# A fused vision block: which PSUM bank each matmul step writes, by strict turn or by an account of when banks are read

## The chip, the cores and the metric

The kernel runs on one core of a Trainium2 chip. The time is the device time of one execution in microseconds. Three executions of the kernel before took 4943.49, 4945.65 and 4948.21 us, so its median is 4945.65 us. Each further execution that was profiled has a span, from its first to its last instruction.

## The reference, cut to what matters

64 images of 3 x 224 x 224 and 64 texts of 77 x 64 come in; 861 tokens of 64 features per image go out. All of it is float32.

```python
p = x.reshape(B, 3, 28, 8, 28, 8).transpose(0, 2, 4, 1, 3, 5).reshape(B, 784, 192)
h = p @ W_embed + b_embed + sin_positional_encoding(784, 64)
for i in range(3):                                  # graph of the 28 x 28 grid
    hw = h @ W_gcn[i]
    agg = hw * snorm; agg = agg.at[:, dst].add(hw[:, src] * enorm)
    h = relu(agg + b_gcn[i])
h = concatenate([h @ W_out + b_out, txt], axis=1)   # 784 + 77 = 861 tokens
a = layernorm(h)
h = h + attention(a)          # 4 heads of 16, softmax over 861 keys, bf16 before Wo
m = layernorm(h)
h = h + shared_mlp(m) + top2_of_4_experts(m)        # 64->64->128->64; 64->128->64->64
```

## The kernel before, in words

The work of an image is cut into steps: tuples such as `("s", g, half, kb, head)`. One list of steps is made on the host for 16 pairs of images at a time (`windows`, `window`), and all five engines walk through that same list in its order, each doing its own part of every step. So the list is the program order of every engine at once. Between the two lists of 16 pairs, all engines meet and the semaphores are cleared.

Where a step stands in the list is set by constants, not by a planner: `image_steps` and `pair_steps` give each group of steps a start and an end in units of images, relative to the image's own scores (0 to 1), `spread` lays the group's steps evenly between them by a rough cost, and `window` sorts everything by that place. With a period of two images, each constant that is a pair of pairs has one value for even and one for odd images. `PACK`, `GRAPH`, `FETCH` place the work of the pair that is coming, up to six images ahead of its scores.

The steps that matter here, with the lines of the profile:

- `s` (PE L1217, one matmul of 432 columns; ScalarE L889 takes the exponential out of PSUM), 56 per image; `pv` (PE L1227, four column groups at once into banks 4 and 5).
- `mx` (PE L1239, one matmul of 432 columns; VectorE L1004 takes the row maximum), 56 per image: the softmax's maximum for the coming image.
- `qk` (PE L1289; ScalarE L910 writes the high part; the step `qkl`, VectorE L1072, then reads the same bank again for the low part) and `gw` (PE L1262; ScalarE L896, then `gwl`, VectorE L1026): banks with two readers, one after the other.
- `gagg` (PE L1271, VectorE L1043), `xt` (PE L1277, ScalarE L905), `v` (PE L1299, VectorE L1082 and L1084), `ot` (PE L1305, VectorE L1091 and L1092), `obt` (PE L1310), `wo` (PE L1316, VectorE L1099), `l1` (PE L1289, ScalarE L952), `l2` (PE L1325 and L1327, ScalarE L958), `wt` (PE L1332, ScalarE L938), `wb` (PE L1339, VectorE L1183), `l3` (PE L1348, ScalarE L962 and L963), `back` (PE L1353, VectorE L1190 and L1191), `embed` (PE L366, VectorE L1018).
- Without PSUM: `xc` (GpSimd L361), the layer norm steps (GpSimd L820 to L837), the expert biases `hb` (GpSimd L847, L852, L857), and the transfers `load`, `fetch`, `text`, `scratch`, `stack` and `store` on the SyncE queue.

PSUM has eight banks. Banks 4 and 5 hold the attention output. The other six, 0, 1, 2, 3, 6 and 7, serve all other matmul steps. `turns` gives each such step its bank: strictly the next of the six. It also gives the number of the bank's use. Before TensorE starts a step it waits until the bank's former user has been read (`pe.wait_ge(free[r], prior)`); every reader waits for `full[r]`. All engines call `turns` on the same list, so they agree.

Of the kernel before, what the change touches and what calls it, by code (L numbers as in the profile page):

```python
# [86 lines left out]
def spread(steps, start, end):  # L87

    def cost(st):
        if isinstance(st, list):  # L90
            return sum(cost(one) for one in st)
        return WAIT * st[1] if st[0] == "wait" else COST.get(st[0], 1)

    total, passed, out = sum(cost(st) for st in steps), 0, []
    for st in steps:
        at = start + (end - start) * passed / total
        out += [(at, one) for one in (st if isinstance(st, list) else [st]) if one[0] != "wait"]
        passed += cost(st)
    return out


def attention_steps(g):
    units = [(half, kb) for half in range(2) for kb in range(NB)]
    out, due = [], []
    for n, unit in enumerate(units):
        for h in range(HEADS):
            out.append(("s", g, *unit, h))
            if h == 1:
                out += due
                due = []  # L110
                if n and n % 2 == 0:
                    out.append([("pv", g, *one) for one in units[n - 2:n]])
                    due = [("oev", g, half) for half, kb in units[n - 2:n] if kb == NB - 1]
    return out + [[("pv", g, *one) for one in units[2 * NB - 2:]], ("wait", 0.1), ("oev", g, 1)]


def max_steps(g):
    out, due = [], []
    for qb in range(NB):
        for h in range(HEADS):  # L120
            for half in range(2):
                out.append(("mx", g, qb, h, half))
                out += due[:1] if half else []
                due = due[1:] if half else due
        due += {3: [("nm", g, 0), ("mrow", g, 0), ("mload", g, 0)],
                NB - 1: [("nm", g, 1), ("mrow", g, 1), ("mload", g, 1)]}.get(qb, [])
    return out + [due[0], ("wait", 0.2), due[1], ("wait", 0.2), due[2]]


def norm_steps(g, which):  # L130

    out = []
    for k in ("sum", "mean", "ln", "wait", "sq", "wait", "var", "ln2", "wait", "scale", "hi", "lo"):
        out.append(("wait", 0.1) if k == "wait" else (k, g, which))
    return out


def finish_steps(g):
    return [("ot", g, 0), ("ot", g, 1), ("wait", 1), ("obt", g), ("wait", 1), ("wo", g)]
# [6 lines left out]
def gate_steps(g):  # L146
    return [("wait", 0.1) if k == "wait" else (k, g) for k in GATE_CHAIN]


def expert_steps(g):  # L150

    out = [("xt", g, "m", 0), ("xt", g, "m", 1), ("wait", 1), ("gate", g)]
    for e in range(EXPERTS + 1):
        out += [("l1", g, e, 0), ("l1", g, e, 1)]
        out += {2: [[("l2", g, 0, 0), ("l2", g, 0, 1)]], 4: [[("l2", g, 1, 0), ("l2", g, 1, 1)]]}.get(e, [])
    return out + [("wt", g), ("l2", g, 2, 0), ("l2", g, 2, 1),
                  [("wb", g, 0, 0), ("wb", g, 0, 1), ("wb", g, 1, 0), ("wb", g, 1, 1)], ("wait", 1), ("l3", g), ("wait", 1),
                  ("back", g)]
# [2 lines left out]


MAX = ((-0.694, 0.158), (-0.638, 0.168))
FINISH = ((0.995, 1.063), (0.994, 1.097))
NORM_M = ((1.109, 1.257), (1.123, 1.197))
EXPERT = ((1.374, 1.997), (1.267, 1.882))
GATE = ((1.492, 1.665), (1.347, 1.379))
BIAS = ((1.602, 1.796), (1.435, 1.621))
NORM_A = ((-1.472, -1.34), (-1.504, -1.457))
PROJECT = ((-1.307, -1.281), (-1.361, -1.284))  # L170
STACK = ((-1.018, -0.911), (-1.082, -0.936))
VALUE = (-0.952, -0.989)

GRAPH = (-2.075, -1.519)
PACK = (-4.037, -3.674, -3.438, -2.779)
VGAP = 0.154
STORE = (2.456, 2.503)
FETCH = -5.787
LOAD_LEAD, EMBED_LAG = 0.117, 0.217


def image_steps(g):
# [3 lines left out]
    def part(steps, times):  # L186
        return spread(steps, g + times[b][0], g + times[b][1])

    project = [("xt", g, "a", 0), ("xt", g, "a", 1), ("wait", 1), ("qk", g, 0), ("qk", g, 1), ("wait", 0.2), ("qkl", g, 0),
               ("qkl", g, 1), ("scratch", g)]  # L190
    return (spread(attention_steps(g), g, g + 1.0) + part(max_steps(g), MAX) + part(finish_steps(g), FINISH)
            + part(norm_steps(g, "m"), NORM_M) + part(expert_steps(g), EXPERT) + part(gate_steps(g), GATE)
            + part([("hb", g, n) for n in range(2 * EXPERTS + 1)], BIAS) + part(norm_steps(g, "a"), NORM_A)
            + part(project, PROJECT) + part([("stack", g, n) for n in range(STACK_PARTS)], STACK)
            + [(g + VALUE[b], ("v", g, 0)), (g + VALUE[b] + VGAP, ("v", g, 1)), (g + STORE[b], ("store", g))])


def pair_steps(p):
# [7 lines left out]
    out = [(t - 1.8, ("text", p))] + spread(graph + [("gw", p, 3, 0), ("gw", p, 3, 1)], t + GRAPH[0], t + GRAPH[1])  # L206
    out.append((t + FETCH, ("fetch", p)))
    for q in range(4):
        out += [((t + PACK[q - 1] if q else t - 2 + PACK[3]) + LOAD_LEAD, ("load", p, q)), (t + PACK[q], ("xc", p, q)),
                (t + PACK[q] + EMBED_LAG, ("embed", p, q))]  # L210
    return out
# [16 lines left out]
def windows(pairs):  # L228
# [4 lines left out]
    while at < pairs:  # L233
# [6 lines left out]
ROTATING = ("s", "embed", "gw", "gagg", "mx", "mrow", "ot", "obt", "wo", "xt", "qk", "v", "gate", "l1", "l2", "wt", "wb", "l3",  # L240
            "back")


def turns(steps):

    count, out = {}, {}
    turn = 0
    for st in steps:
        if st[0] in ROTATING:
            bank = (0, 1, 2, 3, 6, 7)[turn % 6]  # L250
            turn += 1
        elif st[0] == "pv" and st[3] == 0:
            bank = 4 + st[2]
        else:
            continue
        count[bank] = count.get(bank, 0) + 1
        out[st] = (bank, count[bank], count[bank] - 1)
    return out
# [30 lines left out]
def build(nc, pairs, x, txt, edges, plain, split, rows, const, out):  # L289
    ctx = ExitStack()  # L290
    with ctx:
# [400 lines left out]
        def _(sp):  # L692
            def run(steps, base, init):
                turn, nth = turns(steps), ordinal(steps)
                packed_last = latest(steps, "xc")
                for st in steps:
# [69 lines left out]
        def _(pool):  # L766
# [17 lines left out]
            def run(steps, base, init):  # L784
                chain[0] = 0
                made.clear()
                turn, nth = turns(steps), ordinal(steps)
                embed_last = latest(steps, "embed")
                xt_last, lo_last = latest(steps, "xt"), latest(steps, "lo")
# [76 lines left out]
        def _(act):  # L866
            def run(steps, base, init):
                turn, nth = turns(steps), ordinal(steps)
                scratch_last = latest(steps, "scratch")
                hb_no = ranks(steps, lambda st: st[0] == "hb" and st[2] == 2 * EXPERTS)  # L870
# [560 lines left out]
```

## Time and profile before

| | before |
|---|---|
| median of 3 runs | 4945.65 us |
| the profiled execution, its own time | 4939.67 us |
| its span | 4937.9 us |
| mean granted TensorE clock | 0.981 |
| PE (matmul) busy | 4719.4 us, 96% |
| PEld (weight load) busy | 3135.6 us, 64% |
| DVE (VectorE) busy | 3206.6 us, 65% |
| ACT (ScalarE) busy | 2979.3 us, 60% |
| POOL (GpSimd) busy | 1696.6 us, 34% |

Matmuls are pipelined: one of 432 columns is recorded as lasting 0.35 to 0.36 us, and yet the next can start about 0.19 us after it. A TensorE that is shown as busy can therefore still be late between two matmuls. The rows of PEld, the weight loads, are the finer gauge: every matmul has its load, and a load that comes late has its idle time and its releaser beside it.

### The profile page before, as it was taken

How to read it: one execution, taken by the hardware profiler on the slowest of the kernel's cores; microseconds unless marked ns; L12 is line 12 of the kernel's file. 1: busy time of each engine (PE TensorE's matmuls, PEld its weight loads, DVE VectorE, ACT ScalarE, POOL GpSimd, SP SyncE). 2: the span in 40 equal slices, each digit the busy share in tenths (PEclk: the TensorE clock that was granted, in tenths of full speed). 3: DMA queues.
4: the chain of work that ended last, by engine and by line, in shares of the span. 5: the costliest groups of instructions: out<-in, count | busy, mean ns of one | idle time of the engine just before them, and what ended most of it. 6: DMA issues, size and time to landing. Idle time of an engine off the chain costs nothing.

```text
span 4937.9 us, 80911 instructions
## 1 busy us (share of the span) xinstructions
PE 4719.4 (96%) x29262; PEld 3135.6 (64%) x29262; DVE 3206.6 (65%) x7342; ACT 2979.3 (60%) x6161; POOL 1696.6 (34%) x1681
## 2 busy tenths in 40 slices
PE   6599999999999999999999999999999999999997
PEld 4466666666666666666666666666666666666654
DVE  4366666676666666666666666667666667666663
ACT  0156666666566666666656666666666666656665
POOL 3123333334234333334333334333333333423322
PEclk8699999999999999999999999999999999999998
DMA  2433433433433432443332443333333343343220
GB/s 87 102 78 81 87 83 78 90 74 81 87 84 77 90 76 74 90 85 82 81 78 70 90 85 82 80 81 75 82 86 82 80 88 74 83 85 74 34 48 6
DMA packets 193397, 385.98 MB, mean 78 GB/s; under 512 B 74986, under 2 KB 118634, under 8 KB 193002
## 3 DMA queue, kind: packets, MB, share of 16 engines
q1 hardware_dynamic: 191978, 379.91, 34.2%
q8 instruction: 237, 3.88, 0.4%
q14 instruction: 158, 1.29, 0.1%
q10 hardware_dynamic: 1024, 0.89, 0.1%
HBM read 309.13 MB, written 109.26 MB: 85 GB/s over the span
## 4 chain that ended last, share of the span: by engine, by line
PE 74%; DVE 11%; ACT 7%; issue 2%; DMA 2%; POOL 1%; ACTq 0%; SPq 0%; DVEq 0%; another core or an unknown queue 0%; POOLq 0%
PE ps L1227 15%; PE ps L1217 13%; PE ps L1239 12%; PE ps L1271 9%; DVE neg_max_halves L1004 8%; PE ps L1289 6%; PE ps L1327 4%; ACT probs L889 4%; PE ps L1348 3%; PE ps L1262 3%; PE ps L366 2%; PE ps L1277 2%; PE ps L1316 2%; PE ps L1295 1%; DMA image_rows<-image_by_row 1%
## 5 line engine op out<-in xcount | busy, mean ns | idle before, releaser
L1004 DVE TENSOR_REDUCE neg_max_halves<-ps 123x1 f32<-123x432 f32 (+1 forms) x3584 | 2000.9, 598 | 766.9 <-PE ps L1239 751.9
L889 ACT ACTIVATE probs<-ps 123x432 f32<-123x432 f32 x3584 | 1690.9, 542 | 663.7 <-PE ps L1217 626.8
L1239 PE MATMUL ps<-k_stack,q_stack 96*123 96x432 f32 x3584 | 1293.5, 396 | 38.5 <-DMA k_stack<-qk_scratch 22.3
L1217 PE MATMUL ps<-q_stack,k_stack 97*123 97x432 f32 x3584 | 1253.1, 395 | 52.6 <-ACT probs L889 12.5
L1239 PEld LDWEIGHTS ps<-k_stack,q_stack 96*123 96x123 f32 x3584 | 638.7, 186 | 419.1 <-issue 273.2
L1217 PEld LDWEIGHTS ps<-q_stack,k_stack 97*123 97x123 f32 x3584 | 641.8, 186 | 340.1 <-issue 107.7
L1227 PE MATMUL ps<-probs,v_and_one 123*32 123x432 f32 x7168 | 763.3, 540 | 1.6 <-ACT probs L889 1.6
L952 ACT ACTIVATE hidden<-ps,plain_w 128x432 f32<-128x432 f32 x640 | 400.2, 634 | 148.2 <-PE ps L1289 148.2
L1271 PE MATMUL ps<-adjacency,parts_hi 112*128 112x392 f32 x1344 | 463.5, 345 | 3.5 <-DVE parts_lo L1026 3.4
L1271 PE MATMUL ps<-adjacency,parts_lo 112*128 112x392 f32 x1344 | 459.8, 342 | 0.0
L815 POOL TENSOR_TENSOR nodes_T<-nodes_T,dinv_row 128x392 f32<-128x392 f32 x128 | 130.8, 1023 | 846.4 <-ACT nodes_T L901 845.3
L1227 PEld LDWEIGHTS ps<-probs,v_and_one 123*32 123x32 f32 x7168 | 182.5, 110 | 353.5 <-issue 287.2
L820 POOL TENSOR_TENSOR centred_and_squared<-tokens,ln_stats_m 123x448 f32<-123x448 f32 x64 | 59.9, 936 | 980.0 <-DVE ln_stats_m L1058 980.0
L852 POOL TENSOR_TENSOR moe_T<-gate_weights,bias_rows 123x448 f32<-123x448 f32 x256 | 242.9, 949 | 311.9 <-DVE gate_weights L1160 283.3
L1043 DVE TENSOR_TENSOR nodes_T<-ps,dinv_row 128x392 f32<-128x392 f32 x192 | 108.4, 565 | 323.3 <-PE ps L1271 323.3
L857 POOL TENSOR_TENSOR tokens<-tokens,moe_T 123x448 f32<-123x448 f32 x256 | 292.6, 1143 | 32.4
L820 POOL TENSOR_TENSOR centred_and_squared<-tokens_next,ln_stats_a 123x448 f32<-123x448 f32 x64 | 59.9, 935 | 674.7 <-DVE ln_stats_a L1058 674.7
L361 POOL COPY patch_columns<-image_rows 96x392 f32<-96x392 f32 x256 | 235.3, 948 | 94.1 <-DMA image_rows<-image_by_row 73.4
L958 ACT ACTIVATE hidden<-ps,plain_w 128x492 f32<-128x492 f32 (+1 forms) x384 | 234.1, 634 | 51.7 <-PE ps L1327 43.7
L1271 PEld LDWEIGHTS ps<-adjacency,parts_hi 112*128 112x128 f32 x1344 | 255.3, 190 | 6.2 <-issue 3.9
L1262 PE MATMUL ps<-plain_w,nodes_T 128*112 128x128 f32 (+2 forms) x1792 | 243.2, 278 | 14.8 <-POOL nodes_T L815 6.8
L1271 PEld LDWEIGHTS ps<-adjacency,parts_lo 112*128 112x128 f32 x1344 | 255.4, 190 | 1.6
(158 smaller groups left out, 6118.3 us busy)
## 6 DMA issues: line engine op xcount, KB each, us to landing
image_rows<-image_by_row SPq DMA_DIRECT2D x256, 586.9 KB
q_stack<-qk_scratch SPq DMA_DIRECT2D x256, 216.0 KB, 7.9
k_stack<-qk_scratch SPq DMA_DIRECT2D x256, 216.0 KB, 9.1
image_by_row<-in_x SPq DMA_DIRECT2D x192, 196.0 KB
qk_scratch<-parts_hi SPq DMA_DIRECT2D x64, 432.0 KB, 2.9
qk_scratch<-parts_lo SPq DMA_DIRECT2D x64, 432.0 KB, 3.7
out<-tokens SPq DMA_DIRECT2D x64, 215.2 KB
tokens_next<-in_txt SPq DMA_DIRECT2D x64, 19.2 KB
```

The source lines that it names most:

```text
L361: return pool.tensor_copy(XCB[:, b, :, :].rearrange("p g (i j) -> p g i j", j=GRID), src)
L852: ins = pool.tensor_tensor(TMP[:, :, :], GW[:, :, e:e + 1].to_broadcast(shape), row("eb3", e).unsqueeze(1).to_broadcast(shape), ALU.mult)
L857: ins = pool.tensor_tensor(hb, hb, TMP[:, :, :], ALU.add)
L889: act.activation(P[:, (g * 2 * NB + unit) % SLOTS, h, :], T[0:BLK, 0:HW], ACT.Exp, scale=SCALE).then_inc(free[r], 1)
L952: act.activation(H1[e % 3][:, c0:c0 + cn], T[:, 0:cn], ACT.Relu, bias=bias).then_inc(free[r], 1)
L1004: v.tensor_reduce(NM[:, qb * HEADS + h, half:half + 1], T[0:BLK, 0:keys], AX.X, ALU.max, negate=True).then_inc(free[r], 1)
L1217: mm = pe.matmul(T[0:BLK, 0:cn], KS[:, g % 2, h, kb * BLK:(kb + 1) * BLK], QS[:, g % 2, h, c0:c0 + cn], start=True, stop=True)
L1227: pm = pe.matmul(acc[32 * h:32 * h + 32, half, 0:HW], VV[:, g % 2, kb, h, :], P[:, slot, h, :], start=kb == 0, stop=kb == NB - 1, tile_pos ...
L1239: mm = pe.matmul(T[0:BLK, 0:cn], QS[0:SHIFT_ROW, g % 2, h, qb * BLK:(qb + 1) * BLK], KS[0:SHIFT_ROW, g % 2, h, c0:c0 + cn], start=True, st ...
L1262: mm = pe.matmul(T[0:m, at * 128:(at + 1) * 128], HT[:, k * size:k * size + m], rhs, start=True, stop=True)
L1271: mm = pe.matmul(T[:, 0:GHALF], part[:, k, :], adj[:, k, half * GHALF:(half + 1) * GHALF], start=k == 0 and part is UH, stop=k == NG - 1 a ...
L1289: mm = pe.matmul(T[:, 0:cn], wsplit(part, name, e, cols), XS[which][:, c0:c0 + cn], start=part is WH, stop=part is WL)
```

## The change

`turns` no longer takes the next bank in turn. It walks through the list with three counters, one for each of TensorE, ScalarE and VectorE, in units that come to about a tenth of a microsecond, and adds for each step what the tables `TENSOR`, `SCALAR` and `VECTOR` say. A step that needs one of the six banks gets the one whose account of being read is the earliest. A bank with two readers is held until the account has passed the second. GpSimd, the transfers and the waits of a step for data have no account. The number of steps and of instructions is the same, and so are banks 4 and 5.

The constants that place the steps are set anew with it; most move by 0.02 of an image or less, the larger ones are the end of `FINISH` and of `BIAS` for odd images, `VALUE` for even ones, `PACK[3]`, `VGAP` and `STORE` for even ones.

```diff
-FINISH = ((0.995, 1.063), (0.994, 1.097))
+FINISH = ((0.983, 1.063), (0.994, 1.135))
-EXPERT = ((1.374, 1.997), (1.267, 1.882))
+EXPERT = ((1.374, 2.0), (1.267, 1.882))
-BIAS = ((1.602, 1.796), (1.435, 1.621))
+BIAS = ((1.602, 1.796), (1.435, 1.543))
-PROJECT = ((-1.307, -1.281), (-1.361, -1.284))
+PROJECT = ((-1.317, -1.293), (-1.38, -1.303))
-VALUE = (-0.952, -0.989)
+VALUE = (-1.064, -0.985)
-PACK = (-4.037, -3.674, -3.438, -2.779)
-VGAP = 0.154
-STORE = (2.456, 2.503)
-FETCH = -5.787
+PACK = (-4.057, -3.674, -3.446, -2.627)
+VGAP = 0.286
+STORE = (2.575, 2.501)
+FETCH = -5.799
+TENSOR = {"s": 2, "mx": 2, "pv": 9, "embed": 8, "gw": 9, "gagg": 23, "xt": 6, "qk": 4, "v": 5, "gate": 8, "l1": 4, "l2": 9,
+          "wt": 5, "wb": 4, "l3": 27, "ot": 5, "obt": 5, "wo": 12, "back": 4, "mrow": 3}
+SCALAR = {"s": 5, "gw": 5, "relu": 5, "xt": 5, "qk": 5, "mrow": 4, "oev": 5, "obt": 7, "sq": 5, "wt": 7, "gexp": 2, "gexp2": 2,
+          "l1": 5, "l2": 5, "l3": 9}
+VECTOR = {"mx": 5, "nm": 2, "embed": 3, "gwl": 6, "gagg": 5, "sum": 5, "mean": 1, "var": 5, "ln2": 1, "qkl": 6, "v": 7, "ot": 9,
+          "wo": 6, "gate": 4, "gmax": 2, ...
 def turns(steps):
-    count, out = {}, {}
-    turn = 0
+    count, out, held = {}, {}, {}
+    free_at = {bank: n - 6 for n, bank in enumerate((0, 1, 2, 3, 6, 7))}
+    tensor = scalar = vector = 0
     for st in steps:
-        if st[0] in ROTATING:
-            bank = (0, 1, 2, 3, 6, 7)[turn % 6]
-            turn += 1
-        elif st[0] == "pv" and st[3] == 0:
-            bank = 4 + st[2]
-        else:
+        kind, bank = st[0], None
+        if kind in ROTATING:
+            bank = min(free_at, key=lambda b: free_at[b])
+            tensor = max(tensor, free_at[bank]) + TENSOR[kind]
+        elif kind == "pv":
+            bank = 4 + st[2] if st[3] == 0 else None
+            tensor += TENSOR[kind]
+        if kind in SCALAR and (kind, st[2:3]) != ("gw", (3,)):
+            scalar = max(scalar, tensor if bank is not None else 0) + SCALAR[kind]
+        if kind in VECTOR or (kind, st[2:3]) == ("gw", (3,)):
+            vector = max(vector, tensor if bank is not None else 0) + VECTOR.get(kind, 8)
+        if bank in free_at:
+            if kind in ("gw", "qk") and (kind, st[2:3]) != ("gw", (3,)):
+                held[(kind + "l", *st[1:])] = bank
+                free_at[bank] = scalar + 6
+            else:
+                free_at[bank] = scalar if kind in SCALAR and (kind, st[2:3]) != ("gw", (3,)) else vector
+        elif st in held:
+            free_at[held[st]] = vector
+        if bank is None:
             continue
         count[bank] = count.get(bank, 0) + 1
         out[st] = (bank, count[bank], count[bank] - 1)
```

## Rows read from the trace of the kernel before

**Rows 1.** The page's chain that ended last, shares of the span.
```profile
PE 74%; DVE 11%; ACT 7%; issue 2%; DMA 2%; POOL 1%; ACTq 0%; SPq 0%; DVEq 0%; another core or an unknown queue 0%; POOLq 0%
```
**Rows 2.** Busy time by stretch: all of the steady part; one pair of images.
```profile
core 0: us, PE busy (x) PEld busy (x) DVE busy (x) ACT busy (x) POOL busy (x), PEclk, DMA share, GB/s
250.00:4700.00 4450.00, 4358.41 (x27269) 2895.57 (x27271) 2975.35 (x6858) 2804.50 (x5807) 1569.29 (x1565) 1.00 0.36 80
...
2656.90:2803.20 146.30, 143.57 (x903) 95.53 (x902) 98.35 (x228) 92.86 (x192) 52.18 (x52) 1.00 0.37 82
```
**Rows 3.** Timeline (start, length, engine, idle before) around an image's end, 2801 us.
```profile
2801.04 1.34 PEld L1239 LDWEIGHTS ps<-k_stack,q_stack 96*123 96x123 f32 x7 [0.70 <-issue]
...
2801.53 3.68 DVE L1004 TENSOR_REDUCE neg_max_halves<-ps 123x1 f32<-123x429 f32 x7 [1.18 <-PE ps L1239]
...
2802.71 0.40 PEld L1305 LDWEIGHTS ps<-ident_r,attn_T 128*123 128x123 f32 x3 [0.33 <-DVE neg_max_halves L1004]
...
2804.76 0.18 PEld L1217 LDWEIGHTS ps<-q_stack,k_stack 97*123 97x123 f32 x1 [0.33 <-DVE neg_max_halves L1004]
```
**Rows 4.** Timeline after a `qk`, 2699.5 to 2704 us.
```profile
2699.79 2.15 DVE L1004 TENSOR_REDUCE neg_max_halves<-ps 123x1 f32<-123x432 f32 x4 [2.07 <-PE ps L1239]
...
2700.78 0.35 PE L1239 MATMUL ps<-k_stack,q_stack 96*123 96x432 f32 x1
...
2701.73 0.88 ACT L938 ACTIVATE image_rows<-ps 12x861 bf16<-12x861 bf16 x1
2701.84 0.99 PE L1325 MATMUL ps<-hidden,plain_w 128*128 128x492 f32 x2
2701.85 1.24 DVE L1072 SCALAR_TENSOR_TENSOR parts_lo<-ps,plain_w,parts_hi 128x432 fp32r<-128x432 f32 x2
...
2702.57 0.18 PEld L1239 LDWEIGHTS ps<-k_stack,q_stack 96*123 96x123 f32 x1 [0.54 <-DVE parts_lo L1072]
...
2703.14 0.29 PEld L1217 LDWEIGHTS ps<-q_stack,k_stack 97*123 97x123 f32 x2 [0.39 <-DVE parts_lo L1072]
```
**Rows 5.** Timeline after an `l3`, 3005 to 3007 us.
```profile
3005.65 1.63 DVE L1004 TENSOR_REDUCE neg_max_halves<-ps 123x1 f32<-123x429 f32 x3 [1.77 <-PE ps L1239]
...
3005.85 0.47 ACT L963 ACTIVATE moe_T<-ps 64x369 f32<-64x369 f32 x1
...
3006.38 0.18 PEld L1217 LDWEIGHTS ps<-q_stack,k_stack 97*123 97x123 f32 x1 [0.34 <-ACT moe_T L963]
...
3006.38 0.46 PE L1217 MATMUL ps<-q_stack,k_stack 97*123 97x432 f32 x1
3006.68 0.37 PE L1239 MATMUL ps<-k_stack,q_stack 96*123 96x432 f32 x1
3006.88 0.40 PE L1217 MATMUL ps<-q_stack,k_stack 97*123 97x432 f32 x1
```
**Rows 6.** Waits of the weight loads in one pair: us, times, longest.
```profile
PEld ps L1217 <- DVE neg_max_halves L1004: 2.0, 7, 0.5
PEld ps L1217 <- ACT probs L889: 2.0, 6, 0.5
...
PEld ps L1227 <- ACT probs L889: 1.8, 3, 0.7
...
PEld ps L1217 <- DVE parts_lo L1026: 0.8, 2, 0.5
...
PEld ps L1239 <- DVE parts_lo L1072: 0.5, 1, 0.5
...
PEld ps L1289 <- ACT hidden L952: 0.2, 1, 0.2
PEld ps L1305 <- DVE parts_lo L1026: 0.2, 1, 0.2
```
**Rows 7.** Waits of VectorE in the same pair.
```profile
DVE neg_max_halves L1004 <- PE ps L1239: 22.7, 19, 2.4
...
DVE parts_lo L1026 <- ACT parts_hi L896: 6.0, 3, 3.7
```
**Rows 8.** Groups of instructions in the same pair: busy, mean ns, idle before.
```profile
L889 ACT ACTIVATE probs<-ps 123x432 f32<-123x432 f32 x112 | 53.0, 542 | 20.3 <-PE ps L1217 19.2 <-ACT image_rows L916 0.7
...
L361 POOL COPY patch_columns<-image_rows 96x392 f32<-96x392 f32 x8 | 7.3, 936 | 0.0
```

More of the change, by code:

```diff
@@ L241 @@
             "back")
+TENSOR = {"s": 2, "mx": 2, "pv": 9, "embed": 8, "gw": 9, "gagg": 23, "xt": 6, "qk": 4, "v": 5, "gate": 8, "l1": 4, "l2": 9,
[3 more added lines that the diff above has]
+VECTOR = {"mx": 5, "nm": 2, "embed": 3, "gwl": 6, "gagg": 5, "sum": 5, "mean": 1, "var": 5, "ln2": 1, "qkl": 6, "v": 7, "ot": 9,
+          "wo": 6, "gate": 4, "gmax": 2, "gsub": 2, "gsum": 2, "grec": 2, "gprob": 2, "gcmp": 4, "gtie": 2, "gadd": 2, "grank": 3,
+          "gsel": 2, "gsum2": 2, "grec2": 2, "gweight": 2, "part0": 2, "rest0": 2, "part1": 2, "rest1": 2, "part2": 2, "wb": 5,
+          "back": 8}
 def turns(steps):
-    count, out = {}, {}
-    turn = 0
+    count, out, held = {}, {}, {}
+    free_at = {bank: n - 6 for n, bank in enumerate((0, 1, 2, 3, 6, 7))}
+    tensor = scalar = vector = 0
     for st in steps:
-        if st[0] in ROTATING:
-            bank = (0, 1, 2, 3, 6, 7)[turn % 6]
-            turn += 1
-        elif st[0] == "pv" and st[3] == 0:
-            bank = 4 + st[2]
-        else:
+        kind, bank = st[0], None
[18 more added lines that the diff above has]
+        if bank is None:
             continue
```

## The prediction

> **What bounds the kernel now.** I read first the chain that ended last: TensorE holds 74% of it and VectorE and ScalarE 18% together, so a microsecond counts where TensorE is late [rows 1]. The busy times by stretch come next. Between 250 and 4700 us TensorE is shown busy 4358 of 4450 us at a granted clock of 1.00, the full 2.4 GHz, with VectorE at two thirds [rows 2]. That seems to leave 2%. It doesn't, because a matmul's record is longer than its spacing, so I went on to the weight loads. Seven loads in a row for `mx` take 1.34 us [rows 3]; with one load of about 0.18 us that is one every (1.34 - 0.18) / 6 = 0.19 us. Against this dense spacing the loads were busy only 95.5 us of a pair's 146.3 us [rows 2]. (A pair of images is 112 `s` steps, and that stretch holds 112 exponentials [rows 8].)
>
> The waits of the loads in this one pair are the view that decides [rows 6]. Each row names what ended the wait. Where the releaser wrote what the matmul reads (L1227 behind L889, 1.8 us), the wait is for data, and the bank has no part in it. Where an `s` or `mx` matmul waits for a VectorE operation of another step, nothing but the bank can be the reason. I sort these bank waits into two kinds.
>
> - Kind A: the releaser is the reader of a bank that is held long: L1072, L1026, L963, L1191, L1092, L1043. The view has 11 such rows, from 0.8 us (L1217 behind L1026) to 0.2 us (L1305 behind L1026), with 12 waits and 4.2 us together [rows 6].
> - Kind B: the releaser is an ordinary short reader, mostly L1004 or L889. 13 rows, from 2.0 us to 0.2 us (L1289 behind L952), with 31 waits and 10.4 us together [rows 6].
>
> **The change, part by part.** What goes is the strict turn. After a `qk`, the sixth step behind it must take its bank: `mx` waits 0.54 us until L1072 has read it, and the next step 0.39 us for the second one [rows 4]. Other banks were free by then. VectorE's run of four reductions ended at 2699.79 + 2.15 = 2701.94 us, and the last of them was that of the `mx` of 2700.78 us; ScalarE had read the bank of `wt` at 2701.73 + 0.88 = 2702.61 us [rows 4]. The account holds a `qk` bank until its `qkl`, so it should name those banks, and both waits go.
>
> After an `l3` it is otherwise. The load at 3006.38 us waits 0.34 us for L963, which ends at 3006.32; but the first of the next reductions ends at about 3005.65 + 1.63 / 3 = 3006.19 us and the `s` banks wait behind L963 on ScalarE [rows 5]. The best other bank wins some 0.1 us. I count `l3` and `back` (1.2 of the 4.2 us, 3 of the 12 waits) as not regained.
>
> How much of a load's idle time is lost? In the run of `s` and `mx` all of it. In rows 4 less: the two matmuls of 492 columns were still streaming in it. I take two thirds, an estimate between a half and the whole. Kind A then gives (4.2 - 1.2) x 2/3 = 2.0 us per pair. There is a second cost. After the waited-for step at 3006.38 the next matmul starts at 3006.68, 0.30 us later, and the one after that at 3006.88, 0.20 us later [rows 5]: a wait costs 0.1 us more, as the next load begins late. 9 waits give 0.9 us. Kind A: 2.9 us per pair. Its bounds are 0 and 4.2 + 1.2 = 5.4 us.
>
> The Trainium skill ("TensorE: Matmul & The Clock Gate", The mechanism) says of this second cost that a weight load overlaps running matmuls only when its row group differs. All loads here use nearly all rows, so by that rule nothing overlaps, a wait spoils nothing behind it, and the 0.9 us fall away (27 us over the run). The trace speaks against it: matmuls recorded at 0.35 to 0.46 us start 0.20 us apart, with their loads between them [rows 5].
>
> Kind B is the uncertain part. It would be worth 10.4 x 2/3 + 31 x 0.1 = 10.0 us per pair if every wait went. The nearest row on what the order can do is the burst at 2801 us: seven `mx` are issued at once, VectorE needs 3.68 us for them, and the loads behind wait 0.33 us again and again [rows 3]. Seven steps fill six banks; no choice of bank helps, TensorE runs at VectorE's pace. Only where `s` and `mx` are mixed and one reader lags does another bank stand free. I take a tenth, 1.0 us, being nearest to that row; the bounds are -5 us (see the third rival) and 10.0 us.
>
> Places. With the new constants the order on the SyncE queue is the same as before: modulo two images it is `load` 1, `text`, `fetch`, `load` 2, `store`, `load` 3, `scratch`, the eight `stack`, `load` 0, `store`, `scratch`, the eight `stack`, in both. So no DMA is moved past another. `PACK[3]` goes 0.152 image (some 11 us at 73 us an image) later; `load` 0 goes with it and keeps 0.45 image, 33 us, until its `xc`. In this pair `xc` never waited at all (idle 0.0) [rows 8], also for quarter 2, which stands 0.12 image behind its load and now 0.11; that covers it, and if the cover went, a late `xc` would hold GpSimd's queue, the norms and biases behind it. The nine `hb` of an odd image are squeezed into 0.108 image, 8 us; GpSimd is busy 52 of 146 us [rows 2] and absorbs that, with `xc` 2 and a norm behind by at most a few us. `VALUE`, `VGAP` and the end of `FINISH` move `v`, `ot`, `obt` and `wo` by up to 10 us among `s` and `mx`, on TensorE and on the reader alike. Moved into a burst they add waits of kind B, moved out they take some: I put it at zero, with 1 us per pair either way.
>
> The sum: 2.9 + 1.0 + 0 = 3.9 us per pair. The steady part is 4450 / 146.3 = 30.4 pairs: 119 us. The first 250 us and the last 238 I leave as they are. The profiled execution took 4939.67 us with a span of 4937.9; it would become 4821. It lay 6 us under the median of the runs, and from that the forecast is 4945.65 - 119 = 4827, say 4828 us.
>
> **The rivals.** *Kind B goes too.* Where the earliest bank is always right, half of the 10.0 us comes back as well. For it: ScalarE has 20.3 us of waiting for TensorE before its exponentials and VectorE 22.7 us before its reductions in the pair [rows 7, 8], so the readers have room. Against it: the burst [rows 3]. The gain is 2.9 + 5.0 = 7.9 us a pair, 240 us: 4705 us; with a third of B 4757 us. Chance 0.17 for all under 4775.
>
> *Given back.* The regained time is spent before the next burst, since TensorE just arrives earlier at six full banks. Then the waits change their rows and not their sum; 1 us a pair of kind A stays: 4915 us. For it: at 2801 us the reader sets the pace, and seven tenths of the waiting is of kind B. The Trainium skill ("Perfetto Trace Analysis", Optimization Strategy) reads the same gap coming again as a sign that PSUM may be too small, which is this case: more banks would help, another order would not. Rows 3 bear it out for that stretch, rows 4 do not. Chance 0.15 for 4880 to 4936 us, and 0.07 for no change, within 0.2% (10 us, about what can be told from none).
>
> *The account misnames banks, and the kernel gets slower.* It knows no waits for data. VectorE's L1026 waits 6.0 us in a pair for ScalarE's L896 with all reductions queued behind it [rows 7]; the account lets `gwl` start as soon as VectorE's own counter allows. It also books 5 units for a reduction that takes 3.68 / 7 = 0.53 to 0.6 us. Behind a `gwl` it thinks the banks of `mx` read while they are not and gives them to an `s`, though the banks of ScalarE are free. Each such pick costs up to one reduction, about 0.3 us on the mean with its follow-up of 0.1. The strict turn is immune, as it needs no times. The point from which it decides is 3.9 / 0.4 = 10 wrong picks a pair, of some 320; with 22 it loses 5 us a pair, 5095 us at the worst, and with 14 it comes to 4997 us. Against it: VectorE catches up in its 19 idle spells [rows 7], which resets the error. Chance 0.11.
>
> **How the numbers follow.** The forecast's own case, 4775 to 4880 us, has 0.50; kind B going too 0.17; given back 0.15; no change 0.07; slower 0.11. Faster by over 0.2%: 0.50 + 0.17 + 0.15 = 0.82. The range 4740 to 4945 us leaves out about 0.06 below (over half of B's share) and 0.14 above (slower, and the upper half of no change).
>
> **What would show it.** In the changed trace, a pair (112 exponentials) should last some 142.4 us. The waits of the loads behind L1072 and L1026 (0.9 and 1.3 us here) should be nearly gone; those behind L963 and L1191 should stay. The waits behind L1004 and L889 should stay at 8 to 10 us a pair; if they grow by what A loses, it was given back; if loads of `s` wait for L1004 right behind a `gwl`, the account misnames. GpSimd's `xc` should still never wait. A wait for data in place of bank waits (L1227 behind L889, 1.8 us now) growing beyond 4 us, or a clock under 1.00 in the steady part, would be something that I haven't foreseen.

## The result: 2% slower, and the profile after

The changed kernel takes 5042.59 us (median of 6 runs, 5039.73 to 5045.31); the kernel before took 4944.57 us beside it. The ratio is 1.0202, with a 95% interval of 1.0191 to 1.0214. The forecast was 4828 us, with 4740 to 4945 us as its range: wrong in its direction, and by 215 us.

| | before | after |
|---|---|---|
| profiled execution / its span | 4939.67 / 4937.9 us | 5040.31 / 5038.5 us |
| mean granted TensorE clock | 0.981 | 0.955 |
| PE busy | 4719.4 us | 4820.0 us |
| DVE / ACT busy | 3206.6 / 2979.3 us | 3206.2 / 2993.2 us |

VectorE is as busy as before and ScalarE nearly so; TensorE is busy 101 us longer for the same number of matmuls (29262). That points to its clock. The busy times by stretch of the changed kernel, with the columns of [rows 2]:

```profile
core 0: us, PE busy (x) PEld busy (x) DVE busy (x) ACT busy (x) POOL busy (x), PEclk, DMA share, GB/s
250.00:4700.00 4450.00, 4359.66 (x26679) 2908.33 (x26677) 2910.25 (x6715) 2754.95 (x5678) 1539.08 (x1532) 0.97 0.35 79
3614.30:3760.30 146.00, 142.94 (x902) 95.59 (x902) 98.15 (x228) 92.92 (x192) 52.25 (x52) 1.00 0.37 83
3012.40:3162.40 150.00, 147.39 (x902) 98.50 (x902) 98.26 (x228) 93.24 (x192) 52.22 (x52) 0.97 0.36 80
...
3015.00:3025.00 10.00, 10.00 (x56) 6.76 (x55) 5.02 (x11) 4.37 (x8) 0.94 (x1) 0.50 0.80 86
```

Two pairs with the same 902 loads: one lasts 146.0 us at a clock of 1.00, the other 150.0 us at 0.97. The last row is where they differ: for 10 us the granted clock is 0.50, 1.2 GHz in place of 2.4. By the clock records of the trace this comes in nearly every pair, 2.7 us behind the first `s` of the odd image (85 us behind the first `s` of the even one), and mostly lasts 10.2 us. Between 250 and 4700 us the changed kernel has 304 us of half clock. The kernel before has 34 us: seven pieces of 3.4 us, 95 us behind the first `s` of an even image, and one of 10.2 us where the two lists of 16 pairs meet. Each us of it costs (150.0 - 145.9) / 10.2 = 0.40 us.

That gives nearly the whole difference. In pairs wholly at full clock the change won 0.4 us (145.9 against 146.3 us; the changed kernel has only three such pairs), 12 us over 30.4 pairs; the clock took (304 - 34) x 0.40 = 108 us. Sum: 96 of the 101 us between the spans. The other 5 us have not been traced.

The waits of the loads in a pair at full clock, as [rows 6] (line numbers are 28 higher):

```profile
PEld ps L1245 <- ACT probs L917: 2.4, 5, 0.9
...
PEld ps L1255 <- ACT probs L917: 2.1, 5, 0.7
PEld ps L1267 <- DVE neg_max_halves L1032: 2.1, 7, 0.5
...
PEld ps L1245 <- ACT attn_bf_T L958: 0.8, 1, 0.8
...
PEld ps L1267 <- DVE parts_lo L1100: 0.2, 1, 0.2
```

Nothing waits for L1054 (before: L1026) any more, and 0.2 us are left of the waits for the second reader of `qk`. Kind A of the prediction is down from 4.2 to 0.8 us, as foretold. But kind B rose from 10.4 to 12.0 us. Its largest rows are the first and the third; those behind L1032 and L917 grew little (before, behind L1004 and L889: 9.6 us; now 10.0), and 1.4 us of it are waits behind readers that caused none before: of `obt` (0.8, the fourth row), of `v` (0.4) and of `wt` (0.2). So A gave 3.4 us, both kinds together fell by 1.8 us, and the pair got 0.4 us shorter. Part of the rest reappears as idle time for which the profile names no releaser ("issue"): 29.0 us in the pair before, 30.2 us now.

What precedes the fall of the clock is in the timeline of the changed kernel around an even image's end (start, length, engine, idle before), to be laid beside [rows 3]:

```profile
3010.46 0.41 DVE L1110 TENSOR_TENSOR v_and_one<-ps,bias_rows 123x256 f32<-123x256 f32 x1
...
3011.38 0.51 PEld L1333 LDWEIGHTS ps<-ident_r,attn_T 128*123 128x123 f32 x4 [0.39 <-DVE v_and_one L1112]
...
3012.41 0.18 PEld L1245 LDWEIGHTS ps<-q_stack,k_stack 97*123 97x123 f32 x1 [0.33 <-DVE neg_max_halves L1032]
...
3013.54 0.29 PEld L1245 LDWEIGHTS ps<-q_stack,k_stack 97*123 97x123 f32 x2 [0.45 <-ACT probs L917]
...
3014.63 0.18 PEld L1267 LDWEIGHTS ps<-k_stack,q_stack 96*123 96x123 f32 x1 [0.79 <-ACT probs L917]
```

The burst is still there, and now `v` with its two VectorE operations and an earlier `ot` stand in it too. The 6.4 us around `ot`, first of the kernel before and then of the changed one:

```profile
2800.70:2807.10 6.40, 6.10 (x36) 3.66 (x29) 5.50 (x13) 2.64 (x6) 0.00 (x0) 1.00 1.04 137
```

```profile
3008.60:3015.00 6.40, 5.49 (x31) 3.38 (x23) 5.48 (x14) 2.01 (x4) 0.00 (x0) 1.00 1.07 137
```

TensorE issues 31 matmuls in place of 36 and 23 loads in place of 29, at a VectorE as busy as before. Right behind it the clock falls. (These counts alone do not tell whether it falls; see the experiments.) The Trainium skill ("TensorE: Matmul & The Clock Gate", A second HAM failure mode: psum-queue depth-cycling) tells of a kernel in which short idle spells between groups of matmuls, from cycling through PSUM banks, made the clock go to and fro; this trace agrees, with loads late by at most 0.79 us there.

### The profile page after: what moved, and what is told of

Its sections match the earlier page's. It is cut to its first block, busy times and chain, and to the rows that moved or that the text cites. A ratio compares the mean times of both kernels' runs of the same rounds, so it can differ in the third digit from the quotient of the medians.

```text
span 5038.5 us, 80911 instructions
## 1 busy us (share of the span) xinstructions
PE 4820.0 (96%) x29262; PEld 3215.7 (64%) x29262; DVE 3206.2 (64%) x7342; ACT 2993.2 (59%) x6161; POOL 1702.3 (34%) x1681
## 4 chain that ended last, share of the span: by engine, by line
PE 84%; DVE 6%; ACT 3%; DMA 2%; issue 1%; POOL 1%; ACTq 0%; SPq 0%; DVEq 0%; POOLq 0%; another core or an unknown queue 0%
PE ps L1245 16%; PE ps L1267 15%; PE ps L1255 15%; PE ps L1299 9%; PE ps L1317 6%; PE ps L1355 4%; DVE neg_max_halves L1032 4%; PE ps L1376 3%; PE ps L1290 3%; PE ps L1344 2%; PE ps L1353 2%; PE ps L394 2%; PE ps L1305 2%; ACT probs L917 1%; PE ps L1367 1%
## 5 line engine op out<-in xcount | busy, mean ns | idle before, releaser
L1032 DVE TENSOR_REDUCE neg_max_halves<-ps 123x1 f32<-123x432 f32 (+1 forms) x3584 | 2017.9, 599 | 774.7 <-PE ps L1267 756.4
L917 ACT ACTIVATE probs<-ps 123x432 f32<-123x432 f32 x3584 | 1698.6, 541 | 708.7 <-PE ps L1245 673.5
L1267 PE MATMUL ps<-k_stack,q_stack 96*123 96x432 f32 x3584 | 1347.4, 407 | 43.6 <-DMA k_stack<-qk_scratch 22.0
L1245 PE MATMUL ps<-q_stack,k_stack 97*123 97x432 f32 x3584 | 1285.2, 405 | 62.4 <-ACT probs L917 40.9
L1267 PEld LDWEIGHTS ps<-k_stack,q_stack 96*123 96x123 f32 x3584 | 655.4, 191 | 430.6 <-issue 261.3
L1245 PEld LDWEIGHTS ps<-q_stack,k_stack 97*123 97x123 f32 x3584 | 669.6, 192 | 344.5 <-issue 121.4
L1255 PE MATMUL ps<-probs,v_and_one 123*32 123x432 f32 x7168 | 789.6, 558 | 2.0 <-ACT probs L917 2.0
L980 ACT ACTIVATE hidden<-ps,plain_w 128x432 f32<-128x432 f32 x640 | 402.0, 637 | 146.5 <-PE ps L1317 146.3
L1317 PE MATMUL ps<-x_stack_moe,split_hi 128*128 128x432 f32 x640 | 245.2, 383 | 1.0 <-DVE neg_max_halves L1032 0.4
```

Of the source, the lines that this page charges most:

```text
L917: act.activation(P[:, (g * 2 * NB + unit) % SLOTS, h, :], T[0:BLK, 0:HW], ACT.Exp, scale=SCALE).then_inc(free[r], 1)
L980: act.activation(H1[e % 3][:, c0:c0 + cn], T[:, 0:cn], ACT.Relu, bias=bias).then_inc(free[r], 1)
L1032: v.tensor_reduce(NM[:, qb * HEADS + h, half:half + 1], T[0:BLK, 0:keys], AX.X, ALU.max, negate=True).then_inc(free[r], 1)
L1245: mm = pe.matmul(T[0:BLK, 0:cn], KS[:, g % 2, h, kb * BLK:(kb + 1) * BLK], QS[:, g % 2, h, c0:c0 + cn], start=True, stop=True)
L1255: pm = pe.matmul(acc[32 * h:32 * h + 32, half, 0:HW], VV[:, g % 2, kb, h, :], P[:, slot, h, :], start=kb == 0, stop=kb == NB - 1, tile_pos ...
L1267: mm = pe.matmul(T[0:BLK, 0:cn], QS[0:SHIFT_ROW, g % 2, h, qb * BLK:(qb + 1) * BLK], KS[0:SHIFT_ROW, g % 2, h, c0:c0 + cn], start=True, st ...
```

## The experiments

All times are medians; ratios are against the kernel before in the same group of runs, whose medians were 4938.72 to 4944.57 us. "Full pair" is the length of a pair of images wholly at full clock, "half clock" the us between 250 and 4700 in which the clock records of the profiled execution say 0.5. Values marked ~ are from pairs that had a fall, less 0.40 us for each us of it; 148.3 and 148.2 come from a single pair each. `v` back, `FINISH` back and the new `FINISH` alone have two runs each.

| | us | ratio (95%) | full pair | half clock |
|---|---|---|---|---|
| before | 4944.57 | | 146.3 | 34 |
| the change | 5042.59 | 1.0202 (1.0191 to 1.0214) | 145.9 | 304 |
| account, old places | 5077.66 | 1.0270 (1.0253 to 1.0287) | ~149.0 | 174 |
| strict turn, new places | 5130.91 | 1.0385 (1.0369 to 1.0401) | 148.3 | 348 |
| change, `v` back | 5177.61 | 1.0477 (1.0456 to 1.0498) | 148.2 | 410 |
| change, `FINISH` back | 4991.80 | 1.0101 (1.0077 to 1.0125) | 145.8 | 160 |
| change + 12 matmuls | 4963.57 | 1.0051 (1.0035 to 1.0068) | 147.0 | 31 |
| before + 12 matmuls | 4979.20 | 1.0081 (1.0066 to 1.0096) | 147.4 | 48 |
| old places, second reader mended | 4983.91 | 1.0092 (1.0077 to 1.0108) | 146.2 | 120 |
| old places, data account | 4928.91 | 0.9975 (0.9961 to 0.9989) | 145.5 | 85 |
| new places, data account | 4947.50 | 1.0013 (1.0003 to 1.0023) | ~145.4 | 137 |
| change + 4 matmuls | 4950.61 | 1.0021 (1.0012 to 1.0030) | 146.1 | 68 |
| old places, data account + 4 | 4924.70 | 0.9967 (0.9954 to 0.9980) | 145.5 | 58 |
| before, new `FINISH` | 5013.85 | 1.0147 (1.0124 to 1.0169) | 147.1 | 140 |

**The two halves of the change.** The constants of the one kernel with the `turns` of the other:

```diff
 # e1_account_old_places: the changed kernel
-FINISH = ((0.983, 1.063), (0.994, 1.135))
+FINISH = ((0.995, 1.063), (0.994, 1.097))
 ... all places as before
 # e2_turn_new_places: the kernel before
-FINISH = ((0.995, 1.063), (0.994, 1.097))
+FINISH = ((0.983, 1.063), (0.994, 1.135))
 ... all places as in the change
```

> The account of banks alone, all places as before. The changed kernel shows, in 29 of its pairs, one stretch of 10 us just behind the end of an even image in which the granted clock is 0.50; its pairs last 150.1 us with that stretch and 146.0 us without, against 146.4 us before. Theory P (places): the new places thin TensorE's work at that spot and the clock falls; the account by itself is worth little. Then here the clock stays as before (mean 0.98) and the time is 4915 to 4950 us. Theory B (banks): the account's picks make the stalls there and the clock falls with them; then here the mean clock is about 0.955 and the time about 5040 us. My blind forecast of a gain by banks alone would still want 4830 us.

> The new places alone, banks in strict turn. Theory P: the clock falls behind each even image here too, mean clock about 0.95 to 0.96, and the time is 5040 us or more (up to 100 us more, as the waits behind qk and gw stay and the places were not set for the strict turn). Theory B: mean clock 0.98 and a time of 4945 to 4990 us.

Both theories were too simple. Each half alone is slower than both together, and in each the full pair is longer than in the kernel before, by 2.7 and 2.0 us. So the places and the assignment of banks can't be judged apart. The clock is low longest with the new places (348 and 304 us); in so far theory P holds. But with the old places the account takes it from 34 to 174 us as well, so its picks bear on the clock too, as theory B has it. And it is not worth "little", it costs 2.7 us a pair. Where, the timeline of that kernel shows, 28 us into a pair:

```profile
3280.70 0.60 ACT L924 ACTIVATE parts_hi<-ps 112x512 fp32r<-112x512 f32 x1 [0.47 <-PE ps L1290]
...
3281.33 0.69 DVE L1054 TENSOR_TENSOR parts_lo<-ps,parts_hi 112x512 fp32r<-112x512 f32 x1 [3.66 <-ACT parts_hi L924]
...
3282.07 0.29 PEld L1245 LDWEIGHTS ps<-q_stack,k_stack 97*123 97x123 f32 x2 [0.56 <-DVE parts_lo L1054]
...
3283.16 0.29 PEld L1245 LDWEIGHTS ps<-q_stack,k_stack 97*123 97x123 f32 x2 [0.80 <-DVE parts_lo L1054]
```

Two `s` are given the banks of the `gw` just issued, since the account lets VectorE read them at once, though it must wait for L924. That is the mechanism of my third rival.

**Taking back single places of the change.**

```diff
 # e3_new_v_back
-VALUE = (-1.064, -0.985)
-VGAP = 0.286
+VALUE = (-0.952, -0.989)
+VGAP = 0.154
 # e4_new_finish_back
-FINISH = ((0.983, 1.063), (0.994, 1.135))
+FINISH = ((0.995, 1.063), (0.994, 1.097))
```

> The changed kernel with VALUE and VGAP as before: the first v of an even image goes back from 0.064 image ahead of an even image's end to 0.048 behind it. Theory P, v at fault: four short matmuls and two VectorE operations leave the stretch in which TensorE waits for VectorE, the clock stays up, 4925 to 4955 us. If v is not at fault: 5030 to 5050 us as in the changed kernel.

> The changed kernel with FINISH as before: ot starts 0.012 image later in even images, obt and wo earlier in odd ones. Theory P, ot at fault: clock up, 4925 to 4955 us. Not at fault: 5030 to 5050 us. I give v the better chance, since it brings 0.8 us of VectorE's time into its burst and ot only shifts by 1 us.

I had it the wrong way round. With `v` back the kernel is the slowest of all, at 410 us of half clock and a longer full pair; `FINISH` back nearly halves the half clock (304 to 160 us) and leaves the full pair as it is. The new `FINISH` alone in the kernel before shows its part. It does two things: `ot` of even images comes earlier, and `obt` and `wo` of odd images come later.

```diff
 # e12_turn_finish_new: the kernel before
-FINISH = ((0.995, 1.063), (0.994, 1.097))
+FINISH = ((0.983, 1.063), (0.994, 1.135))
```

> The kernel before with the new FINISH alone: ot of an even image begins 0.012 image earlier, obt and wo of odd images later. Taking FINISH back in the changed kernel halved the half-clock time, 304 to 160 us. If ot's place decides by itself, the clock falls here in most pairs: 5000 to 5050 us. If it decides only together with the account's banks or with v, the time is 4940 to 4980 us.

It costs 1.47%: 0.7 us on the full pair (147.07 against 146.35) and 140 us of half clock in place of 34, with a fall 86 to 88 us into 12 of some 30 pairs. The time is in the range for "decides by itself", but the falls come in fewer than half of the pairs, not in most. The falls sit right behind the even image's burst, where the earlier `ot` stands, which speaks for `ot` as their cause; the two moves weren't tried apart. The longer pair is mostly not its doing: in the full pairs of both traces the 17th `s` already starts 0.5 us later, 20 us into the pair, where only the odd image's `obt` and `wo` have moved.

**Is it TensorE's activity that the clock follows?** Needless matmuls, a matmul done twice into the same bank with the same operands, add work and need no further data:

```diff
 # e5_pad_new: the changed kernel; e8_pad_before: the kernel before
-mm = pe.matmul(T[0:BLK, 0:cn], QS[0:SHIFT_ROW, g % 2, h, ...
+for _ in range(2 if g % 2 and qb == NB - 1 else 1):              # mx
+    mm = pe.matmul(T[0:BLK, 0:cn], QS[0:SHIFT_ROW, g % 2, h, ...
-mm = pe.matmul(T[0:BLK, 0:cn], KS[:, g % 2, h, ...
+for _ in range(2 if g % 2 and (half, kb) == (0, 0) else 1):      # s
+    mm = pe.matmul(T[0:BLK, 0:cn], KS[:, g % 2, h, ...
```

> The changed kernel with 12 needless matmuls a pair just where the clock falls: the last eight mx and the first four s of each odd image are done twice into the same bank, same operands. They add at most 12 x 0.19 = 2.3 us to a pair, less where TensorE waits for VectorE anyway. Theory C (the clock falls because TensorE does too little in that stretch): the 10 us at half clock, worth 4.1 us a pair (150.1 against 146.0), go or get shorter; pairs of 146 to 148.3 us, 4920 to 4990 us, faster than the changed kernel's 5043 although it does more. Theory D (the fall has another cause, such as the whole load): the clock falls as before and the time is 5043 to 5110 us.

> Control of the needless matmuls: the same 12 in the kernel before, whose clock falls only for 3.4 us in every third or so pair (1.4 us each). Theory C: that fall, 10 us behind the stretch, goes or stays; the time is 4945 plus 0 to 70 us, minus up to 15. Theory D: 4945 plus 20 to 70 us and the clock as in the kernel before.

What came of it is as theory C has it. The steady part, and the 6.4 us around `ot`, of the changed kernel with 12 matmuls more:

```profile
250.00:4700.00 4450.00, 4373.05 (x27531) 2949.30 (x27529) 2959.04 (x6826) 2802.99 (x5777) 1566.73 (x1560) 1.00 0.35 80
2816.10:2822.50 6.40, 5.93 (x33) 4.33 (x30) 5.69 (x14) 1.83 (x4) 0.00 (x0) 1.00 1.08 133
```

The clock is back at 1.00, the half clock down from 304 to 31 us, and a kernel that does more work is 79 us faster than the change without it. The price of the work is seen at full clock, 147.0 against 145.9 us and in the control 147.4 against 146.3 us: 1.1 us a pair in both, 33 us. The control's half clock did not fall (34 and 48 us): its short falls lie elsewhere, 95 us into a pair, and it just pays the price. By the sum, the changed kernel should win (304 - 31) x 0.40 - 33 = 76 us.

**Is the account too rough, or is there little to win?** First the error just shown, mended; then an account with durations from the trace and with the waits for data, both with the old places:

```diff
 # e6_second_reader_waits: the change's account
-vector = max(vector, tensor if bank is not None else 0) + ...
+vector = max(vector, tensor if bank is not None else 0, first.get(st, 0)) + ...
 held[(kind + "l", *st[1:])] = bank
+first[(kind + "l", *st[1:])] = scalar
 # e7_data_account_old_places: another account
+need = ready(("ot", g, 0), ("ot", g, 1))       # obt; likewise pv, gagg, gw, qk, wo, l2, l3, ...
+need = max(need, free_at[bank])
+tensor = need + 10 if need > tensor else tensor
+start = ready((kind[:-1], *st[1:]))            # gwl, qkl: after ScalarE's part
+vector = max(vector, start) + DVE_.get(kind, 9)
 ...
```

> The account of banks with the old places, mended at one point: the second reader of a gw or qk bank is booked to start only when ScalarE's account has finished the first. With the old places the change's account costs 149.0 us a pair outside the clock's falls against 146.3, and the first 1.2 us of it appear where an s gets a bank of gw that VectorE has not yet read (27.6 and 28.2 us into a pair). Theory M (the misnamed banks of gw are most of it): 1 to 1.5 us a pair come back, 5020 to 5045 us, or less if the clock recovers too. Theory N (the data waits that the account lacks elsewhere, as of obt, matter as much): under 0.5 us come back, 5060 to 5090 us.

> Another account with the old places: durations as the trace of the kernel before has them, in hundredths of a microsecond, and TensorE, ScalarE and VectorE wait in it for the data of their steps too (obt for ot, wo for obt, gagg for gwl, and so on). If my forecast's sum was right and only the change's account is too rough, pairs come to 142 to 144 us and the time to 4830 to 4880 us. If a free bank merely brings TensorE sooner to the next full one (given back), pairs stay at 145.5 to 147 us and the time at 4920 to 4960 us. If the places must be set for the assignment of banks, whatever it is, pairs are 148 us or more and the time is over 5000 us.

The one dependency gives back 94 us, more than theory M wanted: the full pair comes from about 149.0 to 146.2 us. The same place in its timeline (line numbers one higher again):

```profile
3216.39 0.69 DVE L1055 TENSOR_TENSOR parts_lo<-ps,parts_hi 112x512 fp32r<-112x512 f32 x1 [3.66 <-ACT parts_hi L925]
3216.50 0.81 PEld L1246 LDWEIGHTS ps<-q_stack,k_stack 97*123 97x123 f32 x4
```

Four `s` go in a row, without a wait. The better account brings 145.5 us and 4928.91 us, the first kernel here that is faster than before, by 0.25%. It is not 142 us. So misnaming was dear, but naming by this better account is worth only 0.8 us a pair. A pair of this kernel waits behind short readers still:

```profile
PEld ps L1307 <- ACT probs L979: 1.4, 5, 0.5
PEld ps L1329 <- DVE neg_max_halves L1094: 1.3, 4, 0.5
PEld ps L1429 <- DVE neg_max_halves L1094: 1.2, 3, 0.6
```

(L1307 is `s`, L1329 `mx`, L1429 `wb`.) The same account with the new places, and needless matmuls in smaller number:

```diff
 # e9_data_account_new_places: e7's turns in the changed kernel
 # e10_pad4_new, e11_data_account_pad4: the changed kernel, and e7
+for _ in range(2 if g % 2 and qb == NB - 1 and h < 2 else 1):    # mx alone
```

> The account that waits for data, with the new places instead of the old. With the old places it gave 4929 us, pairs of 145.5 us outside the clock's falls. Theory S (places have to be set for one assignment of banks, and these were set for the change's account): worse than the changed kernel outside the falls, 147 us or more, over 5040 us. Theory T (a better account helps with any places; only the strict turn and the misnamed gw banks spoil them): 145 to 146 us outside the falls, the time then hangs on the clock: 4920 if it stays up, up to 5040 if it falls in each pair as in the changed kernel.

> The changed kernel with four needless matmuls a pair instead of twelve: the mx of query block 6, heads 0 and 1, of the odd image, just where the low clock begins. Twelve brought 304 us of half clock down to 31 us and the time from 5043 to 4964 us, at a cost of some 40 us for the work itself by the control. Theory C: if four are enough, the same gain at a third of the price: 4930 to 4945 us. If the fall needs more to be held off, half of the falls stay and the time is 4970 to 5010 us. Theory D (the fall did not hang on the activity): 5043 to 5070 us.

> The account that waits for data with the old places, and the same four needless matmuls. It had 85 us of half clock at 0.4 us each, 35 us in all, mostly 3.4 us pieces 94 us into a pair, 10 us behind these matmuls. If those pieces go too: 4900 to 4915 us, the fastest. If only the falls right behind the burst can be held off this way, the price of some 13 us and a little gain: 4925 to 4945 us.

Theory T holds: at full clock the new places are as good as the old ones for the better account, 145.4 us. With it a short fall of 3.4 us comes in nearly each pair in place of the 10.2 us, 137 us of half clock in place of 304, and the time is within 0.2% of the kernel before. So with the places all new, another assignment of banks alone took away 95 us, most of what the change had cost. Four matmuls do nearly what twelve did, 68 us of half clock at 0.2 us a pair. That they delay the rest by so little makes it unlikely that a mere shift in time, and not the added work, keeps the clock up; no run tested such a shift alone. And with the data account they give the fastest kernel, 4924.70 us, 0.33% under the kernel before; against the same without them, in another group of runs, 4 us are too little to call. The falls some 94 us into a pair mostly stayed, as the second half of that expectation had it.

What in the burst decides is not the number of matmuls. The 6.4 us around `ot` with `v` back, where the clock fell 0.4 us later, and with the four needless matmuls, where it stayed up for another 10 us:

```profile
2926.60:2933.00 6.40, 5.70 (x38) 3.37 (x29) 5.11 (x12) 2.01 (x4) 0.00 (x0) 1.00 1.08 140
```

```profile
2809.40:2815.80 6.40, 5.87 (x31) 3.96 (x27) 5.68 (x14) 2.01 (x4) 0.00 (x0) 1.00 1.08 129
```

With 38 matmuls it fell, with 31 it did not. The shown busy time ordered these two rightly (5.70 and 5.87 us; 5.49 in the changed kernel, 6.10 before), but with the new `FINISH` alone, at 5.95 us, the clock fell behind some bursts and not behind others.

## Why the prediction was wrong

- **What bounds the kernel**, TensorE's lateness: right. The waits named in [rows 6] were real waits for banks.
- **Kind A goes**: right in the changed kernel, 4.2 to 0.8 us. The step from there to time failed: "Kind A: 2.9 us per pair", with 1.0 more for kind B, came out at 0.4 in all, and at 0.8 with the better account. About half of what A gave went into kind B (10.4 to 12.0 us), which I had set to shrink by a tenth. At full clock that is close to my second rival, "given back", with its 1 us a pair; but its reason, the full set of banks in the burst, is shown only in part, as most of the growth stands behind the readers of `obt` and `v` and not behind L1032 and L917.
- **Places, "I put it at zero, with 1 us per pair either way"**: outside its bounds. The new places cost 2.0 us a pair at full clock with the strict turn, and 314 us more of half clock. I had looked at their DMAs and at GpSimd's slack and not at what they do to the burst of [rows 3]. The new `FINISH` alone cost 0.7 us a pair and 106 us more of half clock.
- **The clock** stood in no term, and that failed worst. I had read 1.00 in the steady part [rows 2] and named a lower clock as what I hadn't foreseen. It cost 108 us, more than the whole loss. With the 107 us by which the gain at full clock fell short (12 us in place of 119) it makes up the miss of 215 us, nearly half and half. Rows for it were there: the burst with its waits, and short falls of the clock in about every fourth pair of the kernel before, which the mean of 1.00 rounds away.
- **The third rival**, misnamed banks behind `gwl`: its mechanism is shown, with the old places (94 us for one dependency, clock included). In the changed kernel no load waits for L1054, so there this misnaming isn't the cause. Yet the account's picks have a share in the loss there too, by way of the clock, since another account with the same places is 95 us faster.

What stays open: why the changed kernel needs `v` where it is (with `v` back both the full pair and the clock get worse), which of the moved steps make up the part of the fall that `FINISH` does not, and by which of its picks the account deepens it.

## What to carry to other kernels

When TensorE is fed to within a few per cent, look at the granted clock stretch by stretch, not at its mean, before valuing any shift of steps: a stretch with late loads may be a few matmuls away from 10 us at half speed, and then needless matmuls there can be cheaper than the fall. Where the clock hardly falls they only cost, as in the kernel before. Waits for a buffer that has several readers in turn are a sum that can be named, but removing them may pay little: here 3.4 us of them gave 0.4 us. An assignment worked out by an account has to contain each wait that delays the release; one missing dependency cost more here than all the good picks won.

## What the runs showed of the hardware

- The clock fell here without any long idle spell. In the 6.4 us before the fall TensorE was shown busy 5.49 us, the latest load was 0.79 us late, and VectorE no busier than before.
- The falls in the steady part lasted 3.4, 6.8 or 10.2 us by the clock records (one 13.7 us), and one us of half clock cost 0.40 us of time in the changed kernel. That it is not more is perhaps because part of the stretch waits for VectorE and ScalarE anyway; no run tested this.
- Four matmuls of 0.19 us each in a pair of 146 us took the half clock from 304 to 68 us, at 0.2 us a pair.
